# First pair of a vision tower kernel: tiles 2 and 3 get an instruction order of their own on every engine

## The reference

```python
h = s4d_kernel(log_dt, x, B, inv_A_real, A_imag, 1024)     # 2 * Re(sum over n of C * exp(dtA * l))
h = h + layernorm(h) @ attn_weight.T + attn_bias            # 1024 x 1024
u = layernorm(h)
gates = softmax(u @ Wr.T)                                   # 4 experts
h = h + u @ W.T + b + mix(gates * 2.0, (u @ A.T) @ Bm.T)    # 1024 x 1024 and rank 8 for each expert
```

## Time and profile before

| | |
|---|---|
| median of 3 runs | 790.19 us (789.36 to 791.6) |
| the profiled execution, its own time | 792.11 us |
| its span in the profile | 790.1 us |
| TensorE busy | 736.7 us (93%) |
| VectorE busy | 664.1 us (84%) |
| ScalarE busy | 590.2 us (75%) |
| GpSimd busy | 106.0 us (13%) |

### The profile page before, as it was taken

The page is one execution under the profiler, slowest core; times in us unless marked ns, Lnnn a source line. Parts: engine busy times, 40 slices in busy tenths (PEclk is TensorE's granted clock), DMA queues, the critical chain, the costliest instruction groups (busy, mean ns, idle before and its releaser), DMA issues.

```text
span 790.1 us, 14982 instructions
## 1 busy us (share of the span) xinstructions
PE 736.7 (93%) x5166; PEld 360.9 (46%) x5166; DVE 664.1 (84%) x1228; ACT 590.2 (75%) x979; POOL 106.0 (13%) x94
## 2 busy tenths in 40 slices
PE   2758999998499999999999999999999999999997
PEld 1633444443244444454445444444544454444443
DVE  7799999888879898888888897988888888987463
ACT  6678876788969787978879787879789697875220
POOL 2000032035102010101001020101011010201020
PEclk9998999999899999999999999999999999999999
DMA  7859958768547364554445362545445462636434
GB/s 274 317 106 171 156 135 187 145 126 175 108 80 133 55 140 82 123 99 89 96 98 120 69 143 53 129 94 120 90 90 106 85 134 57 137 65 127 78 79 98
DMA packets 258842, 94.21 MB, mean 119 GB/s; under 512 B 245424, under 2 KB 251440, under 8 KB 258680
## 3 DMA queue, kind: packets, MB, share of 16 engines
q1 hardware_dynamic: 258712, 93.66, 56.8%
q10 hardware_dynamic: 96, 0.13, 0.1%
HBM read 18.26 MB, written 16.78 MB: 44 GB/s over the span
## 4 chain that ended last, share of the span: by engine, by line
PE 75%; DVE 10%; ACT 5%; SPq 4%; DMA 3%; issue 2%; ACTq 0%; DVEq 0%
PE ps_g L723 35%; PE ps_g L877 22%; PE ps_x L877 9%; PE ps_a L714 5%; PE ps_g L884 1%; PE ps_p L914 1%; SPq L453 1%; SPq L436 1%; DMA forms<-in_L_attn_weight 1%; ACT phase L1048 1%; DVE h_tok L1569 1%; DVE wa_lo L1714 1%; ACT L1063 1%; DMA spare<-spare 1%; DVE turn L1503 1%
## 5 line engine op out<-in xcount | busy, mean ns | idle before, releaser
L723 PE MATMUL ps_g<-wa_hi,x 128*128 128x512 f16 x960 | 254.7, 381 | 8.8 <-DMA wa_lo<-residual 7.4
L723 PEld LDWEIGHTS ps_g<-wa_hi,x 128*128 128x128 f16 x960 | 93.1, 98 | 122.6 <-issue 13.5
L723 PE MATMUL ps_g<-wa_lo,x 128*128 128x512 f16 x480 | 145.0, 381 | 0.0
L877 PE MATMUL ps_g<-stage,forms 128*128 128x512 f16 x504 | 115.9, 385 | 8.9 <-DVE residual L1947 8.9
L1080 ACT ACTIVATE junk<-ps_a,stat 128x1024 bf16<-128x1024 f32 x32 | 35.4, 1105 | 68.6 <-DVE stat L1572 68.6
L877 PEld LDWEIGHTS ps_g<-stage,forms 128*128 128x128 f16 x504 | 49.7, 99 | 70.3 <-issue 12.2
L723 PEld LDWEIGHTS ps_g<-wa_lo,x 128*128 128x128 f16 x480 | 47.1, 98 | 56.8 <-issue 0.8
L1612 DVE SCALAR_TENSOR_TENSOR residual<-ps_g,unscale,h_tok 128x1024 f32<-128x1024 f32 x32 | 41.0, 1282 | 36.9 <-PE ps_g L723 36.9
L1947 DVE SCALAR_TENSOR_TENSOR residual<-ps_g,unscale,residual 128x512 f32<-128x512 f32 x84 | 62.7, 747 | 10.1 <-PE ps_g L877 6.4
L877 PE MATMUL ps_g<-wf_hi,forms 128*128 128x512 f16 x224 | 69.0, 379 | 0.9 <-DVE residual L1947 0.9
L1447 POOL TENSOR_TENSOR form_sum<-xn_b 128x512 f32<-128x512 f32 x14 | 18.8, 1344 | 357.5 <-DVE xn_b L1629 357.5
(11 more groups left out here) (287 smaller groups left out, 1348.1 us busy)
## 6 DMA issues: line engine op xcount, KB each, us to landing
out<-residual SPq DMA_DIRECT2D x124, 128.0 KB, 2.2
stage<-in_L_ffn_W SPq DMA_DIRECT2D x8, 512.0 KB, 14.6
x_raw<-in_x SPq DMA_DIRECT2D x38, 64.0 KB
residual<-in_L_attn_weight SPq DMA_DIRECT2D x4, 512.0 KB, 7.3
wf_hi<-in_x SPq DMA_DIRECT2D x1, 2048.0 KB, 9.8
forms<-form_tok SPq DMA_TRANSPOSE x106, 3.2
xn_b<-in_L_ffn_W SPq DMA_DIRECT2D x3, 512.0 KB, 3.8
form_tok<-in_L_ffn_W SPq DMA_DIRECT2D x3, 512.0 KB, 5.4
```

The source lines that it names most:

```text
L723: mm = pe.matmul(ps[:, o, :], x1_part(part, x1_home(t, i))[:, k, :], ws[:, k, o * HALF:(o + 1) * HALF], start=k == 0 and part == 0 and ws ...
L877: mm = pe.matmul(bank, form_part(f, part)[:, k, :], weights(w, k), start=start and k == 0 and part == 0 and w == 0, stop=k == KB // 2 - 1 ...
```

## The change

Nothing is computed otherwise. Tiles 2 and 3 leave the order of the loop and get one of their own.

- VectorE: `low_first(2)` comes before `keep_h(3, 0)` and `low_sums(2)` moves from there to behind `low_m(3, 1)`, just ahead of `keep_h2(2, 1)`. `normalise_1(3, 0)` comes before `make_m(3, 1)`. `low_sums(3)` is cut in two; its first three parts stand ahead of `low_u(3, 1)`. The low parts of S2 and S4 come ahead of `keep_h(3, 1)`. `take_p1` stands right behind `normalise_1(3, 1)`, and `take_p5` ahead of `keep_h2(3, 0)`.
- TensorE: the S4 product (`product_3`) moves from `second_products` to behind `product_6`, ahead of `attn(3, 1)`. `s4(4, 0)` moves into the middle of `attn(3, 1)`.
- ScalarE: `high_first(2)` before `high_sums(2)`; `high_1(3, 0)` before `high_m(3, 1)`; three of the four `high_sums(3)` ahead of `high_u(3, 1)`; the high parts of S2 and S4 and `phases(4, 0)` ahead of the last one; `decays(4, 0)` behind the guess of half (3, 1).
- GpSimd: `sum_weights(3)` waits for `low_1(3, 0)` (`s_lo1`) instead of `attn(2, 1)` (`s_g1`), and `add_other_forms(2)` no longer waits for `s4(3, 1)`.
- SyncE: `turn_first_forms(2)` and `load_again(3)` come before `turn_sums(2)`; the transposes of the sums 3 come before those of the forms S1, A22, S2 and S4, except for T4, which comes last. T4's rows of part 3 use a free quarter of `residual` in place of the space of form S2, so `high_sums` waits there for a store and `keep_h2(3, 1)` for the transpose. The waits of the products on `s_sum_t` are 240 where the last transpose (256) isn't needed.

```diff
             low_u(3, 0)
-            low_sums(2)
+            low_first(2)
             keep_h(3, 0)
             finish(1, 1)
+            normalise_1(3, 0)
             make_m(3, 1)
-            normalise_1(3, 0)
+            low_1(3, 0)
             round_turns(3, 1)
-            low_1(3, 0)
             low_m(3, 1)
-            low_first(2)
+            low_sums(2)
             keep_h2(2, 1, 0)
             make_u(3, 1)
             normalise_2(2, 1, 0)
+            low_sums(3, (T1, T3, T2))
             low_u(3, 1)
             low_form(2, A22, 2)
             low_form(2, S1, 3)
-            low_sums(3)
-
-            pair_step(3, 1, ended=False)
+            low_form(2, S2, 4)
+            low_form(2, S4, 5)
+            low_sums(3, (T4,))
+
+            keep_h(3, 1)
+            make_m(4, 0)
+            normalise_1(3, 1)
+            take_p1(2, 0)
+            round_turns(4, 0)
+            low_1(3, 1)
+            low_m(4, 0)
+            take_p5(2, 0)
+            keep_h2(3, 0, 1)
+            make_u(4, 0)
+            pair_gate_begin(2)
+            normalise_2(3, 0, 1)
+            pair_gate_end(2)
+            low_u(4, 0)
+            take_p6(2, 0)
+            low_form(2, S3, 6)
+            low_first(3)
+            next_h(4, 0, 3, 1, True)
+            keep_h2(3, 1, 1)
+            make_u(4, 1)
+            end_11(2, 0)
+            normalise_2(3, 1, 1)
+            end_12(2, 0)
+            take_p7(2, 0)
+            low_u(4, 1)
...
             product_6(2)
+            product_3(2)
+            pe.wait_ge(s_x1, 32 * (2 * 3 + 1 + 1))
+            pe.wait_ge(s_h2, 2 * 3 + 1)
+            attn_part(3, 1, range(0, KB // 2))
             s4(4, 0)
-            attn(3, 1)
-            second_products(2)
+            attn_part(3, 1, range(KB // 2, KB)).then_inc(s_g1, 1)
+            second_products(2, third=False)
...
                 if j == 3:
-                    pool.wait_ge(s_g1, 2 * FIRST + 2)
+                    pool.wait_ge(s_lo1, 2 * FIRST + 3)
...
-                if beside:
+                if beside and not (isinstance(t, int) and t == FIRST):
                     pool.wait_ge(s_s4, 2 * t + 4)
...
             turn_lora(1, 1)
-            turn_sums(2)
+            turn_first_forms(2)
             load_again(3)
             turn_x1(3, 0)
-            turn_first_forms(2)
+            turn_x(4)
+            turn_sums(2)
             store(1, 1)
-            turn_x(4)
+            turn_sums(3, (T1, T3, T2))
             turn_second_forms(2)
-            turn_sums(3)
+            turn_third_forms(2)
+            turn_sums(3, (T4,))
...
+                high_sums(3, (T1, T3, T2))
+                high_u(3, 1)
+                high_form(2, A22, 0)
+                high_form(2, S1, 1)
+                high_form(2, S2, 2)
+                high_form(2, S4, 3)
+                join_x(4)
+                phases(4, 0)
+                high_sums(3, (T4,))
```

More of the change, by code:

```diff
@@ L206, in sum_tok @@
                 return params[:, HALF:L].bitcast(F16)
-            return forms[:, S2 if f == T4 and j == 3 else 3 + f, :].bitcast(F16)
+            return (residual[:, 1, 1, 0:HALF] if f == T4 and j == 3 else forms[:, 3 + f, :]).bitcast(F16)
         def sum_part(j, f, part):
@@ L531, in turn_sums @@
                     sp.wait_ge(s_wf[1], 128)
-                for f in (T1, T3, T2, T4):
+                for f in chosen:
                     sp.wait_ge(s_sum_lo, 4 * j + f + 1)
@@ L542, in turn_form @@
                     sp.wait_ge(s_g2, 2 * FIRST - 1 if f <= A12 else 2 * FIRST)
-                    if f >= S2:
-                        sp.wait_ge(s_sum_t, 192 if f == A22 else 256)
+                    if f > S2:
+                        sp.wait_ge(s_sum_t, 192 if f == A22 else 240)
                 else:
@@ L664, in step @@
                 turn_second_forms(t)
-            step(3, 1, stored=False)
+            step(3, 1, stored=False, third=False)
             for t in range(4, TILES - 2):
@@ L947, in product_6, with product_3, second_products @@
                 pe.wait_ge(s_taken, EACH * (t - FIRST) + 1)
+                if isinstance(t, int) and t == FIRST:
+                    pe.wait_ge(s_sum_t, 240)
                 add_form(bank_a, S2, added(T2), False).then_inc(s_product, 1)
-            def second_products(t):
+            def product_3(t):
+                pe.wait_ge(s_form_t[S4], 16 * (t - FIRST) + 16)
+                pe.wait_ge(s_taken, EACH * (t - FIRST) + 2)
+                add_form(bank_c, S4, plain(1, 1), False)
+            def second_products(t, third=True):
                 tau = t - FIRST
@@ L963, in second_products @@
                 pe.wait_ge(s_taken, EACH * tau + 4)
+                if isinstance(t, int) and t == FIRST:
+                    pe.wait_ge(s_sum_t, 256)
                 add_form(bank_b, A22, added(T4), True)
@@ L1233, in pair_exp, with high_sums @@
                                    bias=stat_p[:, 1, i:i + 1], accum_out=stat_p[:, 2, i:i + 1]).then_inc(s_pair_exp, 1)
-            def high_sums(j):
+            def high_sums(j, chosen=(T1, T3, T2, T4)):
                 if j == 0:
                     act.wait_ge(s_lbt, 16)
-                for f in (T1, T3, T2, T4):
+                for f in chosen:
                     act.wait_ge(s_sum, 4 * j + f + 1)
                     at_least(act, s_sum_t, 64 * j)
+                    if j == 3 and f == T4:
+                        act.wait_ge(s_out[1], 64 * FIRST)
                     act.activation(sum_part(j, f, 0), sum_rows(j, f), ACT.Copy, scale=scale[:, 1:2])\
@@ L1335, in second_half @@
                 high_form(t, S1, 1)
-                if sums:
-                    high_sums(3)
                 if waves and x:
@@ L1340, in second_half, with first_pair @@
                     waves_ahead(t + 2, 0)
+            def first_pair():
+                square_1(3, 0)
+                rstd_guess(3, 0, stat_1, s_ssq1, s_log1, s_y1, m_eps)
+                high_1(3, 0)
+                high_m(3, 1)
+                split_x(4)
+                sines(3, 1)
+                square_2(2, 1, 0)
+                rstd_guess(2, 1, stat_2, s_ssq2, s_log2, s_y2)
+                high_sums(3, (T1, T3, T2))
[7 more added lines that the diff above has]
+                high_sums(3, (T4,))
+                square_1(3, 1)
+                rstd_guess(3, 1, stat_1, s_ssq1, s_log1, s_y1, m_eps)
+                decays(4, 0)
+                high_m(4, 0)
+                high_1(3, 1)
+                sines(4, 0)
+                phases(4, 1)
+                square_2(3, 0, 1)
+                rstd_guess(3, 0, stat_2, s_ssq2, s_log2, s_y2)
+                pair_exp(2)
+                high_u(4, 0)
+                high_form(2, S3, 4)
+                high_first(3)
+                decays(4, 1)
+                second_half(3, 1)
             step(1, 0, True)
@@ L1351, in _ @@
             decays(3, 1)
-            second_half(2, 0, sums=True)
+            first_pair()
             def pair_step(t, p):
@@ L1609, in keep_h2 @@
                 dve.wait_ge(s_g1, j + 1)
+                if isinstance(t, int) and (t, i) == (FIRST + 1, 1):
+                    dve.wait_ge(s_sum_t, 256)
                 if not isinstance(t, int) or t >= 2:
@@ L1905, in _, with low_sums @@
             low_2(0, 1)
-            def low_sums(j):
-                for f in (T1, T3, T2, T4):
+            def low_sums(j, chosen=(T1, T3, T2, T4)):
+                for f in chosen:
                     dve.wait_ge(s_sum_hi, 4 * j + f + 1)
@@ L2112, in _ @@
             low_form(2, S1, 3)
-            low_sums(3)
-            pair_step(3, 1, ended=False)
+            low_form(2, S2, 4)
[26 more added lines that the diff above has]
+            low_u(4, 1)
+            low_form(3, A22, 2)
+            low_form(3, S1, 3)
+            end_21(2, 0)
             with dve.Fori(2, TILES // 2 - 1) as two:
```

24 lines of the change are left out of this document (11 added, 13 removed).

## The result

The changed kernel takes 793.43 us (median of 20 runs, 791.6 to 794.94) where the kernel before, run beside it, takes 791.64 (20 runs): a ratio of 1.0018, 95% interval 1.001 to 1.0026, so 1.4 us longer. That is a real difference and lies inside 0.3%. The forecast was +2.2 us, 792.4 in a range of 787.0 to 795.0, with 0.38 on "within 0.3%", where the result lies, and 0.43 on "slower by more". The level came out 1.0 us above 792.4 although the shift was 0.8 us smaller, since the kernel before ran at 791.64 beside it and not at the 790.19 that the forecast started from. The profiled execution has a span of 790.9 us.

What follows compares the result with a forecast made beforehand. TensorE was taken as full in the loop, with the gain depending on VectorE's list; early gains and later losses put s4(4, 1) at 242.4 instead of 240.25, +2.2 us on 790.2, giving 792.4 us, range 787.0 to 795.0.

Steps and rivals of the forecast that it cites:

- The rule for VectorE beside GpSimd: Each VectorE instruction with two SBUF inputs meeting a GpSimd subtraction costs 1.08 us, at most one per subtraction; 7 meetings.
- the two bounds: Extra time of low_sums on VectorE when it meets a GpSimd subtraction: 0 or 1.08 us; the prediction took 1.08.
- rival 1: VectorE does not meet GpSimd from 178 to 187 and 193 to 198: -3.0 us, 787.2; chance 16%.
- check by sum: VectorE's time from 168.15 to low_u(4, 1)'s end: 1.5 more from meetings, 0.8 more idle, shift +1.5 at the least.
- To `low_1(3, 0)`: VectorE's list from low_u(3, 0): low_1 ends at 177.9, where it began at 178.81 before; a gain of 2.1 us.
- To `keep_h2(2, 1)`: VectorE up to keep_h2(2, 1), starting at 187.3; TensorE stands 8.1 us and s4(3, 1) comes 7.7 us late.
- the slow clock behind it: Attention of (3, 0) on TensorE: clock falls in the 8.1 us stall, 2.6 us lost.
- Beside it: Sums 3 and forms under the slow attention: last sum ends at 202.3, so the clock costs only about 0.4 us.
- The products: TensorE from keep_h(3, 1): the 8.95 us gap is closed, s4(4, 0) loses 0.2, the attention is over at 229.2.
- The second half: VectorE late: TensorE waits 4.7 us at the A22 product, 2.7 more before s4(4, 1), which starts 2.2 late.
- rival 4: Clock falls again at the 4.7 and 2.7 us waits, or transposes land late: up to 2.6 more, 795.0; chance 15%.
- Rival 2: The gap before the sixth product goes with its slow clock, nothing new comes: 11.6 us gained, 778.6; chance 4%.

Runs made afterwards that it cites:

- experiment 1: The changed kernel with keep_h2(2, 1) ahead of low_sums(2) instead of behind it: 792.75 us against 791.26 for the kernel before, ratio 1.001.
- experiment 2: The changed kernel with GpSimd's sum_weights(3) waiting for keep_h2(2, 1) instead of low_1(3, 0): 792.72 us against 791.26 for the kernel before, ratio 1.0009.
- experiment 3: The changed kernel with product_3(2) back behind the attention of (3, 1): 793.37 us against 791.26 for the kernel before, ratio 1.0017.
- experiment 5: The kernel before with only take_p1(2) moved, right behind normalise_1(3, 1): 790.03 us against 791.26 for the kernel before, ratio 0.9979.
- experiment 4: The changed kernel up to keep_h(3, 1), the old order from there: 795.24 us against 791.49 for the kernel before, ratio 1.0049.
- experiment 7: The kernel before with take_p1(2), take_p5(2) and product_3(2) earlier and s4(4, 0) inside the attention of (3, 1): 791.35 us against 791.49, ratio 1.0003.
- experiment 8: The changed kernel with s4(4, 0) ahead of the whole attention of (3, 1) again: 795.17 us against 792.6 for the kernel before, ratio 1.0033.

## Why the prediction was right, and which of its terms were off

**The rule for VectorE beside GpSimd held.** `low_sums` takes 1.75 us beside a subtraction and 0.75 without, so the upper of the two bounds (1.08) was the one to take, and rival 1 had no ground. Booked time of VectorE alone over the stretch that answers to the earlier trace rows:

```profile
167.64:240.82 73.18, 64.07 (x101) 0.93 0.59 118
```

Its booked time rose by 1.8 us (the check by sum had said 1.5), its idle time by 0.1, 9.0 to 9.1 (the check had said 0.8). Together they are 1.9 us, and the passage is 1.3 us longer. The other 0.6 were slack: before, `low_u(4, 1)` was done at 239.50 (238.28 and 1.22) and TensorE, still at its products, began `s4(4, 1)` at 240.25; now it begins 0.14 us behind `low_u(4, 1)`. The check's "+1.5 at the least" was therefore no lower bound, as the idle time it added did not come. By the Trainium skill's rule (SBUF — State Buffer, "Who interferes with whom") a DVE instruction with two SBUF inputs contends with a GpSimd instruction that reads SBUF, while one with at most one SBUF input does not, outside the modes in which DVE uses two ports. The trace agrees with both halves: `low_sums` 1.75 against 0.75, `keep_h2` 1.27 inside a subtraction in experiment 1. The prediction charged operations with two SBUF inputs alone, and experiment 2 has a row for the condition at the end: the last write of `normalise_2`, a TENSOR_SCALAR with one SBUF tile as input, took 1.55 us beside GpSimd where it takes 0.81. That it ran in such a mode was not tried.

**"To `low_1(3, 0)`" and "To `keep_h2(2, 1)`" held.** On this profile's clock, which is 0.5 us behind that of the earlier trace rows, `round_turns`, right behind `low_1(3, 0)`, began at 177.28 (forecast 177.9) and `keep_h2(2, 1)` at 186.44 (187.3), and the stall was 7.70 us (8.1).

**The term that was mis-sized is the slow clock behind it.** The step charged 2.6 us, the slow stretch behind the earlier trace rows's gap. The attention of (3, 0) took 199.81 - 187.87 = 11.94 us where it took 194.14 - 183.67 = 10.47 before: 1.5 us. The clock came back about 3 us after work began, not after 5.2. With it `s4(3, 1)` ended at 201.24, and `keep_h(3, 1)` at 201.75 came right behind the last sum. Put on the clock of the earlier trace rows that is 202.3, where the forecast had 203.4; the last sum's own end was forecast to the tenth (202.3). "Beside it" had named this: were the clock kept, the sums would be next in line. They were. The 0.4 us that it gave for the cost of the clock at the end does not follow from its own steps, which have 203.4 against 202.3, so 1.1; measured, the slow clock cost nothing there. From `keep_h(3, 1)` to `s4(4, 1)` the forecast had 39.0 us and the profile shows 39.3, so the whole difference between +2.2 and +1.3 came in here.

**"The products" held.** `take_p1` ran from 206.11 and the sixth product waited for nothing, `take_p5` at 211.48 was ahead of the third product. `s4(4, 0)` was expected to lose 0.2 us and lost none. The 1.18 us ahead of the gates' inputs, for the transpose of a form, were not foreseen. They are on the chain, as the chain above shows, but as VectorE stood only 0.23 us for `s4(4, 0)`, they can have cost little.

**"The second half" held, with its two waits out of proportion.** The A22 product waited 3.70 us (forecast 4.7) and `s4(4, 1)` 1.15 (2.7). The clock fell a second time at the first of them, the mechanism of rival 4: the product took 4.44 us instead of 2.75. It cost nothing, as `s4(4, 1)` waited for `low_u(4, 1)` all the same, and experiment 3 shows it from the other side, with the product at full clock and `s4(4, 1)` no earlier beyond the noise of D.

**Rival 2, the whole visible loss of 11.6 us as a gain, is settled by experiment 5.** It narrows the gap to 3.43 us and gains about 2, since `low_u(4, 0)` comes next at once. "Whether it does depends on VectorE" was the right question.

**Why the change loses at all.** The front costs 3.9 us (experiment 4) and the back gains 2.5 of them back. The two parts do not simply add: on the old front the takes, the third product and the split together gain nothing (experiment 7, 1.0003), since the split there undoes the 3.6 us of the rest. What of the back helps behind the new front is so far known only for the split (experiment 8) and the third product (experiment 3, nothing). For the 3.9 the chain of the changed kernel suggests the cause: the sums 2, late and slowed by GpSimd, hold back their transposes, ScalarE, the sums 3, the forms and with them `keep_h(3, 1)` at the end of the list. Experiments 1 and 2 each undo one piece and win 0.6 to 0.7 us by the ratios, which the intervals do not tell from the changed kernel; D says 0.95 and 0.44, the second no more than its noise. So most of the 3.9 us is not shown by an edit, and how it splits between the move of `low_sums(2)` itself and the transposes' new order was not tried.

## What to carry to other kernels

The largest stall on the bounding engine need not be on the chain: taking away 5.6 of its 7.70 us was worth 0.6, while 2.7 us of wait in experiment 5 counted in large part. So before a queue is rewritten to close a gap, ask what the engine would wait for next, and follow the chain of waits rather than the idle time. When an order changes in several places, time each part by itself and then together: the kept order with two takes moved and one product pulled forward was 3.6 us faster than before, and the whole change 1.4 slower. The split of the attention cost 3.8 us on one front and not on the other. An operation moved on VectorE also moves what it meets on GpSimd, here mostly at about 1 us for each meeting of an operation with two SBUF inputs.

## What the runs showed of the hardware

The length of a wait of TensorE did not by itself tell its price in clock. Waits of 1.81 us (experiment 3) and 2.99 left the granted clock at full, and waits of 3.27 to 7.46 us ahead of the 12 matmuls of a product left them at 4.42 to 5.28 us instead of 2.75, the 7.46 (experiment 4) at 4.42 and the 3.75 (experiment 7) at 5.28. And a wait of only 2.71 us, close behind such a product, left `s4(4, 0)` at 2.61 instead of 1.49 (experiment 5). The fall can also come after work has resumed: in experiment 5 the clock fell at about 209.1, 0.5 us into the product that had waited 3.43 us. In the first stall of the changed kernel it was at half from about 184.1, 3.9 us after TensorE's last matmul, and back about 3 us after work resumed; in the kernel before it fell 4.5 us into the gap and was back 5.8 us after work resumed (214.48 to about 220.2). So one slow stretch cost 1.5 us in one place and 2.6 in the other, 2.9 with the 0.24 that it took from the `s4(4, 0)` behind, and a forecast should carry both.
